# One shared-expert group split around the routed experts, and the carried state applied in two full-width products

## The reference

```python
x = x + attn(layernorm(x), Wq, Wv, q_norm_w, v_norm_w)
x = x + ffn(layernorm(x), Wg, W1, W2, W3, Ws1, Ws2, Ws3)

# attn: 16 heads of 16; K is the normalised input itself
Q = rms_norm_multihead(X @ Wq.T) ; V = rms_norm_multihead(X @ Wv.T)
W = cumsum(einsum('blhd,blhe->blhde', K, V), axis=1)
out = einsum('blhd,blhde->blhe', Q, W)

# ffn: 32 experts, 4 per token, expert width 128; shared expert width 256
y = sum over the token's 4 experts of weight * (silu(x@W1[e]) * (x@W3[e])) @ W2[e]
z = (silu(x@Ws1) * (x@Ws3)) @ Ws2
return y + z
```

## Time and profile before

| | |
|---|---|
| time, median of 3 runs | 570.58 us (570.04 to 571.71) |
| time of the profiled execution | 570.52 us |
| its span (first to last instruction) | 568.8 us |
| PE busy | 540.5 us, 95% |
| DVE busy | 360.4 us |
| ACT busy | 367.4 us |
| POOL busy | 331.8 us |
| moved by DMA | 123.26 MB, mean 217 GB/s |

### The profile page before, as it was taken

The page is one execution under the profiler, slowest core; times in us unless marked ns, Lnnn a source line. Parts: engine busy times, 40 slices in busy tenths (PEclk is TensorE's granted clock), DMA queues, the critical chain, the costliest instruction groups (busy, mean ns, idle before and its releaser), DMA issues.

```text
span 568.8 us, 17659 instructions
## 1 busy us (share of the span) xinstructions
PE 540.5 (95%) x4793; PEld 375.6 (66%) x4793; DVE 360.4 (63%) x1353; ACT 367.4 (65%) x1258; POOL 331.8 (58%) x367
## 2 busy tenths in 40 slices
PE   6899999999999998798999999999999999979996
PEld 3465666666666664366888888888888885534554
DVE  7698999999999994751333333333333336843886
ACT  3687999898999974303666666666666665643452
POOL 6010477677777777751655565565566564447991
PEclk8999999999999999797999999999999999979999
DMA  8998365555565545935777766666666654419997
GB/s 243 318 292 292 115 224 205 203 217 200 201 228 197 213 181 188 361 115 142 221 212 216 216 199 180 187 186 171 189 184 180 181 181 144 142 67 398 409 406 265
DMA packets 65085, 123.26 MB, mean 217 GB/s; under 512 B 9824, under 2 KB 44000, under 8 KB 64992
## 3 DMA queue, kind: packets, MB, share of 16 engines
q1 hardware_dynamic: 47824, 78.07, 43.5%
q0 software_dynamic: 13056, 39.86, 19.1%
q10 hardware_dynamic: 4112, 4.19, 2.2%
HBM read 58.49 MB, written 63.60 MB: 215 GB/s over the span
## 4 chain that ended last, share of the span: by engine, by line
PE 79%; issue 4%; POOL 4%; DVE 4%; SPq 3%; DMA 2%; ACT 2%; ACTq 1%; POOLq 0%; DVEq 0%
PE pS L965 20%; PE pQV L830 10%; PE pS L981 9%; PE pS L743 8%; PE pS L797 5%; PE pO L890 5%; POOL xs L471 4%; PE pQV L947 3%; PE pO L871 3%; PE pT L947 2%; PE pT L776 2%; PE pO L805 2%; SPq L389 2%; DMA xg<-xs 1%; PE pQV L759 1%
## 5 line engine op out<-in xcount | busy, mean ns | idle before, releaser
L499 POOL DMA_INDIRECT ys<-gsh,dst x144 | 138.1, 959 | 118.8 <-ACT gsh L666 99.6
L471 POOL DMA_INDIRECT xs<-xg,posi x128 | 123.8, 967 | 52.1 <-issue 31.4
L965 PE MATMUL pS<-w,after_a 128*128 x512 | 134.1, 385 | 0.0
L965 PEld LDWEIGHTS pS<-w,after_a 128*128 128x128 f32 x512 | 88.4, 193 | 7.3
L981 PE MATMUL pS<-w,after_a 128*128 x256 | 76.6, 381 | 0.0
L665 ACT CAST dst<-xg 128x1 int32 x128 | 24.5, 191 | 76.8 <-PE pS L981 75.0
L1077 DVE TENSOR_TENSOR w<-pS,tri 128x512 f32<-128x512 f32 x96 | 64.9, 677 | 1.4 <-PE pS L797 1.4
L830 PE MATMUL pQV<-w 128*128 128x512 f32 x128 | 63.3, 617 | 0.5 <-ACT w L537 0.5
L1342 DVE COPY after_a<-pT 128x128 f32<-128x128 f32 x72 | 21.0, 292 | 67.3 <-PE pT L970 67.1
L1342 DVE COPY after_a<-pO 128x128 f32<-128x128 f32 x72 | 21.0, 292 | 66.6 <-PE pO L970 65.9
L666 ACT ACTIVATE gsh<-pS,xg 128x256 f32<-128x256 f32 x128 | 60.7, 474 | 0.2 <-issue 0.2
(11 more groups left out here) (222 smaller groups left out, 1096.0 us busy)
## 6 DMA issues: line engine op xcount, KB each, us to landing
xg<-xs SPq DMA_DIRECT2D x128, 160.0 KB, 2.5
ys<-gsh SPq DMA_DIRECT2D x32, 512.0 KB
w<-ys SPq DMA_DIRECT2D x32, 512.0 KB, 15.2
w<-in_L_ffn_W ACTq DMA_DIRECT2D x1, 4096.0 KB
out<-xall SPq DMA_DIRECT2D x14, 256.0 KB, 6.3
xs<-padrow SPq DMA_DIRECT2D x32, 80.0 KB
xg<-xs SPq DMA_DIRECT2D x32, 80.0 KB, 2.2
ys<-gsh,dst POOLq DMA_INDIRECT x144
```

The source lines that it names most:

```text
L471: pool.indirect_dma_start(out=xs, out_offset=bass.IndirectOffsetOnAxis(ap=posi[:, a.r8, k:k + 1], axis=0), in_=xr[:, a.r8, :], in_offset=N ...
L499: pool.indirect_dma_start(out=ys, out_offset=bass.IndirectOffsetOnAxis(ap=dst[:, j % 8:j % 8 + 1], axis=0), in_=y[:, j % 8, :], in_offset= ...
L965: last = pe.matmul(pS[a.b][:, 0:2 * F], xgT[:, a.b, k, :], w13_of(e, k), start=(k == 0), stop=(k == KC - 1))
```

## The change

Two things are changed. First, the fourth shared group (g = 3) is taken apart. Its half (0, 0) is issued before the expert pipeline, (0, 1) after the transposes of block 0; ACT applies the silu before its copy of block 1, and DVE multiplies in place in sg (a new semaphore `kept`), since gsh is taken by y. The halves (1, 0) and (1, 1) stand in the last two steps in which the pipeline transposes a gated product (blocks 142 and 143), into pT0 and pQV. After the pipeline DVE only copies sg to gsh and gates the second half; PE issues the four halves of group 4 with no wait between them, then `shared_z(3)`, then groups 5 to 7 as before. Second, line 871 becomes one 128 x 128 product for each half of the channels instead of four of 32 output columns, and moves ahead of the router product (860).

```diff
         early = {(1, 0, 0): pQV, ...
-                 (2, 1, 0): pS[3], (2, 1, 1): pT1}
+                 (2, 1, 0): pS[3], (2, 1, 1): pT1, (3, 0, 0): pS[2], (3, 0, 1): pS[3],
+                 (3, 1, 0): pT0, (3, 1, 1): pQV}
@@ ACT
             def expert_step(tile_of):
                 if (a := tile_of(0)) is not None:
+                    if a.t == 1:
+                        half_silu(NPRE, 0)
...
             def copy_parts(t):
                 wait(act, S["parts_sum"], t + 1)
+                if t == 0:
+                    act.wait_ge(S["silu_done"], FC * NPRE + 2)
...
-            half_silu(3, 0)
             half_silu(3, 1)
@@ PE, attention: this block now stands before the router product
-                    for g in range(KC):
-                        for j in range(4):
-                            at = g * P + 32 * j
-                            last = pe.matmul(pO[32 * j:32 * j + 32, g * P:(g + 1) * P], w_bd[:, a.b, at:at + 32], qT[:, a.b, g, :],
-                                             start=(g == 0), stop=False, skip_group_check=True)
+                    for g in range(KC):
+                        last = pe.matmul(pO[:, g * P:(g + 1) * P], w_bd[:, a.b, g * P:(g + 1) * P], qT[:, a.b, g, :],
+                                         start=(g == 0), stop=False, skip_group_check=True)
                     last.then_inc(S["o1_ps"], 1)
@@ PE, experts
                     last.then_inc(S["xT_ps"], 1)
+                    if a.t == 0:
+                        shared_half(NPRE, 0, 1)
                 if (a := tile_of(3)) is not None and mixed(a.t):
+                    if a.t == NJ - 2:
+                        pe.wait_ge(S["xT_done"], NJ)
+                        shared_half(NPRE, 1, 0)
+                    if a.t == NJ - 1:
+                        shared_half(NPRE, 1, 1)
...
+                    if a.t == 0:
+                        pe.wait_ge(S["silu_done"], FC * NPRE + 1)
+                    if a.t == 1:
+                        pe.wait_ge(S["kept"], 1)
...
+            shared_half(NPRE, 0, 0)
             pipelined(NJ, 4, expert_step)
...
-            for g in range(NPRE, NG):
+            shared_half(NPRE + 1, 0, 0)
+            shared_half(NPRE + 1, 0, 1)
+            shared_half(NPRE + 1, 1, 0)
+            shared_half(NPRE + 1, 1, 1)
+            shared_z(NPRE)
+            for g in range(NPRE + 2, NG):
                 for m in range(FC):
                     shared_h(g, m)
-                if g > NPRE:
-                    shared_z(g - 1)
+                shared_z(g - 1)
             shared_z(NG - 1)
@@ DVE
+            dve.wait_ge(S["silu_done"], FC * NPRE + 1)
+            dve.tensor_tensor(sg[:, 0, :], sg[:, 0, :], h_bank(NPRE, 0, 1)[:], ALU.mult).then_inc(S["kept"], 1)
...
-            half_gate(3, 0)
+            dve.wait_ge(S["kept"], 1)
+            dve.tensor_copy(gsh[:, NPRE % 2, 0, :], sg[:, 0, :]).then_inc(S["gsh_done"], 1)
             half_gate(3, 1)
```

More of the change, by code:

```diff
@@ L315, in build @@
             cnt_ps tabs pads_known spare_stored tab_blk row_ps erow_done brow_done
-            xT_ps xT_done hb_ps sge_done ge_done gT_ps gT_done y_ps y_done parts_sum parts_copied half_sum added summed s_copied masked_pool padded w13_staged w2_staged y2_done""".split()
+            xT_ps xT_done hb_ps sge_done ge_done gT_ps gT_done y_ps y_done parts_sum parts_copied half_sum added summed s_copied masked_pool padded w13_staged w2_staged y2_done kept""".split()
         S = {n: sem(n) for n in names}
@@ L850, in step @@
                               ).then_inc(S["rank_ps"], 1)
+                if (a := tile_of(2)) is not None:
+                    wait(pe, S["qT_done"], a.t + 1)
+                    wait(pe, S["state_done"], a.t)
+                    wait(pe, S["x2_done"], a.t)
+                    for g in range(KC):
+                        last = pe.matmul(pO[:, g * P:(g + 1) * P], w_bd[:, a.b, g * P:(g + 1) * P], qT[:, a.b, g, :],
+                                         start=(g == 0), stop=False, skip_group_check=True)
+                    last.then_inc(S["o1_ps"], 1)
                 if (a := closing(tile_of(5))) is not None:
@@ L863, in step @@
                     last.then_inc(S["lgT_ps"], 1)
[L864 to L867, removed]
-                    for g in range(KC):
-                        for j in range(4):
-                            at = g * P + 32 * j
-                            last = pe.matmul(pO[32 * j:32 * j + 32, g * P:(g + 1) * P], w_bd[:, a.b, at:at + 32], qT[:, a.b, g, :],
-                                             start=(g == 0), stop=False, skip_group_check=True)
-                    last.then_inc(S["o1_ps"], 1)
                 if (a := tile_of(2)) is not None and a.t < NT - 1:
```

## The result

The changed kernel took 574.5 us (570.68 to 578.63, 22 runs) and the kernel before 572.18 us (569.96 to 575.75, 22 runs) beside it: ratio 1.0044, 95% interval 1.0026 to 1.0062. That is 0.44% or 2.5 us slower, and above the range, which ended at 572.6. The profiled execution took 572.83 us, with a span of 570.6. Further on both kernels were run and profiled again in a later session (`unchanged`, `changed_again`). The table takes both pairs apart at eight marks; each figure is the change of a stretch, after minus before, from the starts of the instructions in the traces.

The account below looks back on a forecast made before the run. A PE-ACT-DVE loop bounds attention, PE the experts (1.62 us a block), transfers the last part. 568.8 + 1.2 − 1.4 + 2.3 − 3.7 = 567.2 us span, plus 1.7: 568.9, taken as 568.8; range 565.8 to 572.6.

Parts of the forecast that it names:

- two gains and two costs: Attention product +1.2 us, halves at the experts' start −1.4, halves at the experts' end +2.3, last part −3.7.
- The half at the start: Halves (0, 0) and (0, 1) before the experts fill PE's idle holes and keep its clock up: −1.4 us.
- what is won at the start stays won: Experts: PE's 1.62 us a block is the stage's pace, so the 1.4 us gained at their start is kept.
- The drain: End of the experts: halves (1, 0) and (1, 1) delay the last blocks and ACT's last scaling: +2.3 us.
- The last part: After the last scaling: PE is about 8 us ahead, transfers become the bound: −3.7 us, between 1.7 and 5.2 gained.
- The product: Line 871 in attention: full-width form adds 0.09 us in every second step, +1.3 us in all, taken as +1.2.
- 0.11 us for every pass: Line 871: each of the new product's four passes takes 0.11 us, so it streams in 0.44 us.
- 14 pairs: Attention: some 14 pairs of tiles run at the steady pace, each 0.09 us longer, +1.3 us.
- The rival that the weight loads show in full: Attention: full-width product shows its weight loads, 0.39 us a pair, 573.1 us in all; 15%, nearly all slower.
- the one that fewer records gain something: Attention: the product's exchange gains because fewer records are issued, some 565.5 us in all; 10%.
- That rule alone: Attention product: equally many mode changes before and after, so the edit gives 0; neutral rival 567.6 us, 15%.
- The slower side that I gave 15%: Whole kernel above 572.3 us, by the full-width product's weight loads in attention, 573.1 us; 15%.

Follow-up runs that it names:

- group_only_c: Kernel before with only the shared group's edit, the attention product left as it was: 573.22 us, ratio 1.0035, in a session at 571 us.
- change_pads: Whole change with the 32 padding-row stores spread over 96 blocks instead of 48, and the wait for their landing moved along: 572.38 us, ratio 1.0019 to the kernel before.
- before_pads_b: Kernel before with the padding-row stores spread over 96 blocks instead of 48, second measurement, in a session at 676 us: 673.66 us, ratio 0.9952.
- attn_only_c: Kernel before with only line 871's edit (full-width product, moved ahead of the router product), in a session at 571 us: 571.87 us, ratio 1.0005.
- before_pads: Kernel before with the 32 padding-row stores spread over 96 blocks instead of 48, in a session at 571 us: 568.94 us, ratio 0.9962.
- z_early: Kernel before with the shared group's edit and all four z additions of group 3 right behind half_gate(3, 1) in DVE's list: 689.2 us, ratio 1.0072.
- z_mid: Kernel before with the shared group's edit; z additions 12, 13 behind half_gate(3, 1), 14, 15 behind half_gate(4, 0): 689.76 us, ratio 1.0078.
- attn_wide: Kernel before with line 871 as two full-width products at the old place, behind the router product: 573.04 us, ratio 1.0034.
- group_only_b: Kernel before with only the shared group's edit, second measurement, in a session at 685 us: 688.67 us, ratio 1.0072.
- after: The changed kernel with both edits, as first measured and profiled against the kernel before: 574.5 us, ratio 1.0044.

## Why the prediction was wrong

The forecast was 568.8 us with two gains and two costs; 574.5 came. The edit of the group was to give −1.4 + 2.3 − 3.7 = −2.8 us and cost 2.0 (`group_only_c`). Step by step:

- **The half at the start: right, then lost.** PE's timeline and the clock came as worked out (block 0 at 257.27, block 5 1.1 to 1.3 us nearer to the last scatter). The step that failed is "what is won at the start stays won", which rested on PE's 1.62 us as the stage's pace. SP, whose queue I had not costed, needs some 1.57 us a block up to block 48 at its quickest and took 1.68. The gain was gone there, and another 0.8 to 1.0 us with it. `change_pads` shows it for the stretch (70.03 us instead of 72.3 and 73.3), in one profile. It is the largest single miss among the terms of the group edit: +1.8 and +2.2 us where I had nothing.
- **The drain: right.** +2.26 us in both pairs of profiles, +2.3 predicted; with the halves moved out, −2.7 and −2.9.
- **Between the last scaling and the first load: a term that the sum did not have.** +0.8 and +1.0 us. A 16 KB instruction transfer lies in it in each profile with the group edit, and in none without; no run moved it alone, so this cause is argued, not shown. `before_pads_b` speaks against it as the whole cause: it needs 4.07 us there without such a transfer, where the other profiles without the group edit need 3.3 to 3.6.
- **The last part: right in kind, too large.** −2.5 and −3.0 us instead of −3.7, and only some −0.6 against `attn_only_c` and `before_pads`. Rate and bytes were right (42.5 × 395 GB/s, then 382). From 20.97 MB at these rates the transfers need 42.5 + 10.9 = 53.4 us and the part lasted 55.7, so what lies around them is 2.3 us where I allowed 0.8. I missed PE's wait for `add_z`, and it does not matter (`z_early`, `z_mid`): what is late next is the transfers, as forecast.
- **Blocks 48 to 143: a term left out.** +0.6 and +2.1 us in the pairs. The four profiles of 571 us that have the group edit's halves in the pipeline need 161.5 to 163.8 us there, the others 159.9 to 162.1. With spread stores left out it is 161.5 to 162.2 against 159.9 to 161.4. Single steps of 2.3 to 3.0 us stand around blocks 129, 137, 140 and 143 in kernels with and without the edit (2.96 us at block 136 in the kernel before). Whether the edit shifts these or it is chance stays open.
- **The product: mis-sized, and partly given back.** From line 849 to the increment I had 0.89 us and it is 0.95; a pair costs 0.19 us instead of 0.09, the stage 2.4 to 2.6 instead of 1.2. The start behind line 849 (0.10 us) and the change behind the product (0.09) came as worked out. The term that failed is 0.11 us for every pass: it holds for three of the four, and the first takes 0.18 us. The kernel before showed this in the row next to the one that I took: line 776 needs 0.27 us for two passes. Besides, 14 pairs do not fit the 143 us that I gave the steady pace; at 12.27 us they are 12. The rival that the weight loads show in full (0.39 us a pair) was too high, and the one that fewer records gain something may have had a part: about 1.6 us at the start of the program, and 0.55 to 0.8% of the time on the slower kind of chip, which no row of the kernel before could have told. By the Trainium skill, "TensorEngine Tiling (Array Packing)", section "Key Properties", a change of mode drains the engine; `attn_wide`, with two changes more, agrees (1.12 us against 0.95). That rule alone gave 0 for this edit; the step grew by 0.15 us with one change both before and after, so it does not cover the case.

No rival as written came true. The slower side that I gave 15% had the wrong mechanism: not 0.39 us a pair for weight loads, but several small terms, most of them of the group edit. That its 573.1 us stands near the 574.5 is chance.

## What to carry to other kernels

A gain at the start of a stage is kept only if no other queue has the same pace: cost every issuing engine per block, SP with its register loads and its odd stores too, before calling one engine the bound. Work that is put into the drain of a pipeline costs most of its length, if the first instruction of the next stage waits for the last result (2.3 of 3.4 us here). When the price of an instruction is taken from a neighbour in the trace, take one that stands behind the same kind of work, and read all such neighbours: the first pass of a group can cost more than the rest. A form with fewer instructions can lose in the steady state and still gain elsewhere.

## What was not expected of the hardware

- PE can stand idle inside a group that waits for no semaphore. On a chip of 571 us it happened rarely (1.29 us in `unchanged` at 51.26). On those of 676 and 685 us it comes in a series in every pair of tiles, and a pair takes 18.2 to 18.9 us instead of 12.3. The Trainium skill, "Runtime: NRT & Kernel Launch", section "Instruction fetch mechanics", says that instructions come in blocks of 16 KB through a queue of the engine's own and that the cost of crossing from one to the next is mostly hidden. The 16 KB transfers are in the traces, and they are no slower where PE stops: from 100 to 200 us eight of 0.9 to 1.7 us in `group_only_b`, 14 of 0.9 to 1.6 us in `unchanged`. Whether the fetch of instructions makes the stops no run shows.
- One program takes 18 to 20% longer in some sessions than in others (676 and 685 us against 571), and some 80 us of the 105 to 115 lie before the last table scatter. Why, and whether it belongs to the chip, these runs don't say.
- The first pass of a full-width float32 product of 128 rows by 128 columns takes 0.18 us behind short 16-bit passes (`after`) and 0.21 behind the blocked router product (`attn_wide`), the passes behind it 0.11. A change from full-width to blocked work costs 0.09 us more.
- Spreading 32 stores of 80 KB over twice the blocks made the kernel 0.4% and 0.5% faster in two sessions, the wait for their landing moved along with them.
